# Causal masking of the first layer's attention: a GpSimd select on the exponentials instead of mask matmuls

## What is computed

```python
q_rope = _rotary_apply(x @ W_q_rope, cos, sin)
scores = jnp.einsum('bqhd,bkhd->bhqk', q, k)
scores = scores + jnp.einsum('bqr,bkr->bqk', q_rope, k_rope)[:, None]
scores = scores / scale
causal = jnp.triu(jnp.ones((Tt, Tt), dtype=bool), k=1)
scores = jnp.where(causal[None, None], -jnp.inf, scores)
w = jax.nn.softmax(scores, axis=-1)
attn = jnp.einsum('bhqk,bkhd->bqhd', w, v).reshape(Bb, Tt, D_MODEL)
return attn @ W_o
```

## Time and profile before

| | us |
|---|---|
| median of 3 runs | 988.91 |
| lowest, highest | 984.66, 989.62 |
| the profiled execution | 987.88 |
| its span, first to last instruction | 986.1 |
| first layer's attention, quads 4 to 63 | 93.9 to 322 |
| dense experts | 322 to 560 |
| second layer's attention | 580 to 845 |
| routed experts and output | to 986 |

### The profile page before, as it was taken

One profiled execution on the slowest core, in us unless ns is written; L12 is line 12 of the kernel. 1 busy time (PEld: TensorE's weight loads), 2 busy tenths in 40 slices (PEclk: granted clock), 3 DMA queues, 4 the chain that ended last, 5 costly groups with the idle time before them and its releaser, 6 DMA issues. The chain is left out here.

```text
span 986.1 us, 13424 instructions
## 1 busy us (share of the span) xinstructions
PE 817.1 (83%) x4532; PEld 519.6 (53%) x4532; DVE 657.8 (67%) x1354; ACT 521.0 (53%) x938; POOL 289.5 (29%) x227
## 2 busy tenths in 40 slices
PE   3567999999998899999989899789889999527850
PEld 2234555665564677777767644345444444226740
DVE  3135567676664586776867697688998886347852
ACT  1013455555546677777767626556556566317740
POOL 3452530311300100000004264772453452133425
PEclk9999999999999999999999969989999999859985
DMA  4253211111110292000002103210010100011003
GB/s 128 47 94 80 72 34 35 34 27 41 31 23 1 80 285 63 0 1 1 1 9 54 46 1 101 63 34 18 26 37 18 47 15 7 6 54 57 31 33 85
DMA packets 56415, 44.84 MB, mean 45 GB/s; under 512 B 6598, under 2 KB 47259, under 8 KB 56347
## 3 DMA queue, kind: packets, MB, share of 16 engines
q1 hardware_dynamic: 55323, 41.88, 16.3%
q0 software_dynamic: 1024, 2.10, 0.7%
HBM read 14.73 MB, written 14.55 MB: 30 GB/s over the span
## 5 line engine op out<-in xcount | busy, mean ns | idle before, releaser
L881 ACT ACTIVATE ring<-single 128x512 f32<-128x512 f32 (+3 forms) x512 | 255.6, 517 | 261.3 <-PE single L1084 143.6
L1496 DVE TENSOR_REDUCE mneg<-pair 128x2 f32<-128x1024 f32 (+3 forms) x256 | 259.6, 1022 | 84.4 <-PE pair L1084 55.7
L1082 PE MATMUL single<-q_op,k_op 104*128 104x512 f32 (+3 forms) x512 | 223.4, 449 | 15.5 <-ACT ring L881 10.7
L1082 PE MATMUL pair<-k_op,q_op 96*128 96x512 f32 (+3 forms) x512 | 185.3, 436 | 31.7 <-DVE mneg L1496 17.5
L747 POOL TENSOR_SCALAR k_op<-k_stk,cst 104x512 fp32r<-104x512 f32 x64 | 99.7, 1573 | 272.1 <-DMA k_stk<-hl 254.5
L1082 PEld LDWEIGHTS single<-q_op,k_op 122*128 122x128 f32 (+1 forms) x512 | 100.6, 197 | 91.6 <-ACT ring L881 65.0
L1082 PEld LDWEIGHTS pair<-k_op,q_op 120*128 120x128 f32 (+1 forms) x512 | 106.1, 212 | 49.2 <-DVE mneg L1496 25.0
L1140 PE MATMUL p_o<-ring,vaug 128*9 128x512 f32 (+3 forms) x1024 | 116.4, 527 | 0.9 <-ACT ring L881 0.9
L908 ACT ACTIVATE ring<-pair,cols 128x512 f32<-128x512 f32 x136 | 86.0, 684 | 35.3 <-PE pair L1184 29.6
L1551 DVE TENSOR_TENSOR ring<-ring,single 128x1024 f32<-128x1024 f32 x60 | 73.3, 1221 | 46.0 <-ACT ring L908 44.8
L1556 DVE TENSOR_TENSOR hid_lo<-ring,hid_hi 128x1024 fp32r<-128x1024 f32 x68 | 84.1, 1237 | 22.7 <-ACT hid_hi L923 19.7
(11 more groups left out here) (293 smaller groups left out, 1301.1 us busy)
## 6 DMA issues: line engine op xcount, KB each, us to landing
xs<-zero SPq DMA_DIRECT2D x10, 1024.0 KB, 10.2
q_op<-hl SPq DMA_DIRECT2D x96, 64.0 KB, 2.0
stage<-in_L_ffn_W_dram SPq DMA_DIRECT2D x8, 512.0 KB, 4.4
stage<-in_L_ffn_rW_dram SPq DMA_DIRECT2D x6, 512.0 KB, 5.8
k_op<-hl SPq DMA_DIRECT2D x48, 64.0 KB
...
```

The lines of the kernel that those rows point to most:

```text
L881: exp_done.by(act.activation(ring[:, n % 8, lo:T], singles[n % 2][:, lo:T], ACT.Exp), (L, n))
L1082: ins = pe.matmul(dst[:, lo:hi], r32(lhs[:, lhs_lo:lhs_lo + P]), r32(rhs[:, lo:hi]), start=True, stop=L == 1)
L1496: s_taken.by(dve.tensor_reduce(mneg[:, G % 2, qt, 2 * p:2 * p + 2], pairs[m % 2][:, :, 0:hi], axis=AX.X, op=ALU.max, negate=True), (L, m))
```

## The change

- Exp units of the first layer lose their mask matmul. The upper triangle of the diagonal tile gets an unmasked exponential, and POOL then sets it to 0: cut_half(Q, half) is one affine_select over two heads' diagonal tiles in ring, 128 partitions x 2 x 128, in place. It waits for the second of its two exponentials. values(Q) waits for the second select of its quad instead of the last exponential.
- values(Q - 1) stands behind exp unit 2 instead of exp unit 1 in the first layer, behind the parts "b". ACT's out_rows stands behind the fourth exponential instead of before it.
- Max units with qt 0 or 1, whose two heads have 256 columns each, write both heads into one bank. One mask matmul of 2 x 128 columns serves both. Units with qt 2 or 3 stay as they were.
- POOL's work is interleaved: behind each half quad's select stands at most one step, a quarter of a rope_copy (two heads of q or k) or a third of a piece of weights (the rounded copy, and the subtraction in two halves). Before, the first four pieces were split ahead of quad 0, and all by quad 10; now it begins in quad 3 and ends in quad 23. The piece loads on SP's queue are spread accordingly between the transfers of operands and maxima.
- The table B_MT goes, and the constants are 128 columns narrower.

The diff, cut to its core:

```diff
+WEIGHT_STEP = {at: n for n, at in enumerate([(0, k) for k in (*range(6, 16), *range(20, 24), *range(28, 32))]
+                                            + [(1, k) for k in range(4, 16)])}
...
+        def unit_scores(L, m):
+
+            pair = pairs[m % 2]
+            return pair[:, 0, :].rearrange("p (i k) -> p i k", i=2) if L == 0 and m % 4 < 2 else pair[:, :, :]
...
             for r in range(NB):
                 G = NG * r
                 m_dma(0, G + 1)
+                head_dma(G + 3)
                 if r == 0:
-                    for n in range(4, 8):
-                        expert0(n)
-                head_dma(G + 3)
+                    expert0(4)
                 if r < NB - 1:
                     rope_dma(r + 1)
+                if r == 0:
+                    expert0(5)
                 m_dma(0, G + 2)
                 if r == 0:
-                    for n in range(8, len(PIECE0)):
-                        expert0(n)
+                    expert0(6)
                 if r < NB - 1:
                     head_dma(G + 4)
                 m_dma(0, G + 3)
+                if r == 0:
+                    expert0(7)
                 if r < NB - 1:
                     head_dma(G + 5)
+                    if r == 0:
+                        expert0(8)
                     m_dma(0, G + 4)
                     head_dma(G + 6)
+                if r == 0:
+                    expert0(9)
...
-            def rope_copy(G):
+            def rope_copy(G, w, half):
                 r, s = G // NG, G % 3
-                pool.wait_ge(rope_rows, R_ROWS * (r + 1))
-                if G >= 3:
-                    exp_done.wait_ge(pool, (0, 16 * (G - 3) + 15))
-                apart(pool)
-                dst = slice(GH * s, GH * s + GH)
-                pool.tensor_copy(r32(q_op0[0:96, dst, :]), qk_rope[:, 0:1, :].broadcast_to([96, GH, T]))
-                rope_set.by(pool.tensor_copy(r32(k_op0[0:96, dst, :]), qk_rope[:, 1:2, :].broadcast_to([96, GH, T])), G)
-
-            def weights0(n):
+                if (w, half) == (0, 0):
+                    pool.wait_ge(rope_rows, R_ROWS * (r + 1))
+                    if G >= 3:
+                        exp_done.wait_ge(pool, (0, 16 * (G - 3) + 15))
+                    apart(pool)
+                at = GH * s + 2 * half
+                ins = pool.tensor_copy(r32((q_op0, k_op0)[w][0:96, at:at + 2, :]), qk_rope[:, w:w + 1, :].broadcast_to([96, 2, T]))
+                if (w, half) == (1, 1):
+                    rope_set.by(ins, G)
+
+            def weights0(n, step):
                 which, lo, hi = PIECE0[n]
-                pool.wait_ge(staged0[n % 4], 16 * (n // 4 + 1))
-                src = stage0[:, n % 4, 0:hi - lo, :]
-                steps.step(pool.tensor_copy(r32(w0[:, which, 0, lo:hi, :]), src))
-                split0.by(pool.tensor_tensor(r32(w0[:, which, 1, lo:hi, :]), src, w0[:, which, 0, lo:hi, :], ALU.subtract), n)
+                mid = (lo + hi) // 2
+                if step == 0:
+                    pool.wait_ge(staged0[n % 4], 16 * (n // 4 + 1))
+                    apart(pool)
+                    steps.step(pool.tensor_copy(r32(w0[:, which, 0, lo:hi, :]), stage0[:, n % 4, 0:hi - lo, :]))
+                elif step == 1:
+                    pool.tensor_tensor(r32(w0[:, which, 1, lo:mid, :]), stage0[:, n % 4, 0:mid - lo, :], w0[:, which, 0, lo:mid, :], ALU.subtract)
+                else:
+                    split0.by(pool.tensor_tensor(r32(w0[:, which, 1, mid:hi, :]), stage0[:, n % 4, mid - lo:hi - lo, :], w0[:, which, 0, mid:hi, :],
+                                                 ALU.subtract), n)
...
+            fill = pool.to_reg(0.0)
+
+            def cut_half(Q, half):
+
+                kc = Q % NT
+                exp_done.wait_ge(pool, (0, GH * Q + 2 * half + 1))
+                at = (GH * Q + 2 * half) % 8
+                tri = ring[:, at:at + 2, P * kc:P * (kc + 1)]
+                cut.by(pool.affine_select(tri, tri, [[0, 2], [1, P]], ALU.is_ge, fill, base=0, channel_multiplier=-1), (Q, half))
+
             for G in range(3):
-                rope_copy(G)
-            for n in range(8):
-                weights0(n)
-            rope_copy(4)
-            for n in range(8, len(PIECE0)):
-                weights0(n)
-            rope_copy(5)
-            rope_copy(6)
-            pool.wait_ge(loads[4], n_load[4])
-            pool.tensor_scalar(by_dim(w_q[1][:, :]), by_head(w_qkv[:, 0:D]), SCALE1, None, ALU.mult)
-            pool.tensor_copy(by_dim(w_k1[:, :]), by_head(w_qkv[:, D:2 * D]))
-            pool.wait_ge(cols_ready, 1)
-            pool.tensor_copy(b_cols[:, :, 0:4], cols[:, R_B1:R_B1 + C1].rearrange("p (e c) -> p e c", c=4))
-            pool.tensor_copy(b_cols[:, :, 4:5], cols[:, R_B2:R_B2 + E1].unsqueeze(2)).then_inc(pool_set, 1)
-            for G in (8, 9, 10, 12, 13, 14):
-                rope_copy(G)
+                for w, half in ((0, 0), (0, 1), (1, 0), (1, 1)):
+                    rope_copy(G, w, half)
+            for r in range(NB):
+                for k in range(8 * NG):
+                    cut_half(4 * NG * r + k // 2, k % 2)
+                    if k < 4 and r:
+                        rope_copy(4 * r + 2, k // 2, k % 2)
+                    elif 16 <= k < 20 and r < NB - 1:
+                        rope_copy(4 * r + 4, k // 2 % 2, k % 2)
+                    elif 24 <= k < 28 and r < NB - 1:
+                        rope_copy(4 * r + 5, k // 2 % 2, k % 2)
+                    elif (r, k) in WEIGHT_STEP:
+                        n = WEIGHT_STEP[r, k]
+                        weights0(n // 3, n % 3)
+                    elif (r, k) == (2, 8):
+                        second_weights()
...
-                    if q % NT == 0 and Q:
+                    if L and q % NT == 0 and Q:
                         out_rows(L, Q // NT - 1)
                     for name, b in beside_quad(s, q, "b"):
                         part(name, b)
                     exp(L, Q, 3)
+                    if L == 0 and q % NT == 0 and Q:
+                        out_rows(L, Q // NT - 1)
...
-            def scores(L, dst, lhs, rhs, lhs_lo, lo, hi, diagonal, mask):
-                ins = pe.matmul(dst[:, lo:hi], r32(lhs[:, lhs_lo:lhs_lo + P]), r32(rhs[:, lo:hi]), start=True, stop=L == 1)
-                if L == 0:
-                    ins = pe.matmul(dst[:, diagonal:diagonal + P], id_bf[:, :], bfc[:, mask:mask + P], start=False, stop=True)
-                return ins
...
+                both = unit_scores(L, m)
                 for i in range(2):
                     qs, ks = operands(L, G, 2 * p + i, 24)
-                    ins = scores(L, pairs[m % 2][:, i, :], qs, ks, P * qt, 0, hi, P * qt, B_MS)
+                    ins = pe.matmul(both[:, i, 0:hi], r32(qs[:, P * qt:P * (qt + 1)]), r32(ks[:, 0:hi]), start=i == 0 or L == 1 or qt >= 2, stop=L == 1)
+                    if L == 0 and qt >= 2:
+                        ins = pe.matmul(both[:, i, P * qt:P * (qt + 1)], id_bf[:, :], bfc[:, B_MS:B_MS + P], start=False, stop=True)
+                if L == 0 and qt < 2:
+                    ins = pe.matmul(both[:, :, P * qt:P * (qt + 1)], id_bf[:, :], bfc[:, B_MS:B_MS + P].unsqueeze(1).broadcast_to([P, 2, P]),
+                                    start=False, stop=True)
...
-                st_full.by(scores(L, singles[n % 2], ks, qs, P * kc, lo, T, P * kc, B_MT), (L, n))
+                st_full.by(pe.matmul(singles[n % 2][:, lo:T], r32(ks[:, P * kc:P * (kc + 1)]), r32(qs[:, lo:T]), start=True, stop=True), (L, n))
 
             def values(L, Q):
                 G, kc = Q // NT, Q % NT
-                exp_done.wait_ge(pe, (L, GH * Q + GH - 1))
+                if L:
+                    exp_done.wait_ge(pe, (L, GH * Q + GH - 1))
+                else:
+                    cut.wait_ge(pe, (Q, 1))
...
                         exp_unit(L, Q, j)
+                        if Q and j == (2, 1)[L]:
+                            values(L, Q - 1)
                         if j == 1:
-                            if Q:
-                                values(L, Q - 1)
                             for name, b in beside_quad(s, q, "b"):
...
-                s_taken.by(dve.tensor_reduce(mneg[:, G % 2, qt, 2 * p:2 * p + 2], pairs[m % 2][:, :, 0:hi],
+                s_taken.by(dve.tensor_reduce(mneg[:, G % 2, qt, 2 * p:2 * p + 2], both[:, :, 0:hi],
                                              axis=AX.X, op=ALU.max, negate=True), (L, m))
```

20 lines of the change are left out of this document (14 added, 6 removed).

## The result

The changed kernel takes 1004.3 us (median of 4 runs, 1001.2 to 1005.0) against 986.8 for the kernel before (4 runs, 984.2 to 989.6): a ratio of 1.016, interval 1.013 to 1.019, which is called 16 us below (the medians lie 17.5 apart). The prediction had 970. The profiled run of the changed kernel took 1004.1 us with a span of 1002.4.

The account below looks back on a forecast made before the run. TensorE's instruction stream was taken to bound the first layer's attention. Groups with norms gave 11.9 us, light groups 7.2, groups 2 and 3 nothing, group 0 0.5, less 1 for SP: 18.6 off 987.9, predicted 970, range 955 to 990.

Parts of the forecast that it names:

- the supply: First layer's attention: TensorE time freed by masks removed or merged, 2.3 us a group, 37 us over 16 groups.
- wide quads: First layer's attention: two or three pair units, 0.5 to 0.7 us each, cover the value matmuls' wait for selects.
- the bounds of the select: One GpSimd select over 256 columns: 0.40 to 0.96 us by other GpSimd rows, 0.75 taken.
- SP's order: Expert pieces spread on SP's load queue: one stands ahead of row maxima quad 16 needs, 1 us charged once.
- slow selects: Rival, chance 0.16: GpSimd selects of 1.3 us make the attention slower, 10.6 us lost, 998.
- groups 2 and 3 over 15 us, the selects are slow: Sign in the first layer's attention: these groups, forecast at about 13.8 us, exceeding 15 would mean slow selects.
- the loop binds: Rival, chance 0.09: TensorE's 19.4 us of waits for exponentials grow as masks go; gain under 5 us, 985.
- The moved values: Value matmuls one score matmul later, waiting for the second select: TensorE idles about 0.4 and 0.3 us between key tiles.
- the second rival: VectorE takes over, chance 0.15: queueing reductions eat 1 us more of each group with norms; gain 11.6, 977.
- GpSimd's second price: Select latency in the first layer's attention: value matmuls wait for their quad's second select, some 10 us in all.
- The clock is no rival: First layer's attention: clock granted 1.00 with TensorE 95% busy, 90% expected after; no clock loss charged.
- the move of the copy of p_o: ScalarE's 0.59 us copy, behind key tile 0's fourth exponential: TensorE waits about 0.4 us once a group.

Follow-up runs that it names:

- the kernel with the one reduction: The changed kernel with the rounded maxima mrow written by a one-element maximum (TENSOR_REDUCE) instead of a copy: 995.3 us, ratio 1.0078 to the kernel before.
- The kernel free of the port wait: The changed kernel with four one-input reductions in place of the copy and subtraction that split the turned maxima: 993.4 us, ratio 1.0061 to the kernel before.

## Why the prediction was wrong

**What held.** The place of the supply; that value matmuls would be covered in wide quads; the bounds of the select (0.407 within 0.40 to 0.96, though 0.75 was taken); the stages outside. SP's order cost nothing where 1 us was charged: no row of the stage waits for a transfer. The rival with the right sign, slow selects at 998, came near the measured time by luck, for a reason that is false: by the prediction's own sum the measured 0.407 should have given 960. So the sign "groups 2 and 3 over 15 us, the selects are slow" misled too: they took 16.7 and 16.8 with fast selects. (The 1.0 us between the profiled run and the median was added to 970 but not to 978 and 998; nothing hangs on it.)

**1. The supply, 2.3 us a group, 37 in all.** In groups at full clock TensorE's busy time falls by 1.5 us a group without the single masks, where 2.0 were counted, and by 0.35 with the two-head masks, about the 0.3 counted: 1.8 a group. The step from a distance between neighbours in a packed row to 16 a group was the error, since a mask ahead of a value matmul or a wait has another price. The larger error was the overlap: the sum let nearly all of it through, and of the 1.5 only 0.8 arrived, because TensorE then waited for exponentials and maxima. Over the whole kernel 7 us came from the 256 single masks. The rival "the loop binds" came nearest: it let under 5 us through of 37, and had 0.09.

**2. The moved values, priced at the select's latency only.** The prediction walked what the third score does ahead of the values and forgot what the values had stood in front of: mt, which waits for the split of the maxima. The order alone costs 6 us (ratio 1.0059), and taking it back in the changed kernel brings 12 of 16. VectorE now leads TensorE's waits, which was the sign of the second rival, but that rival had queueing reductions in mind and a kernel faster than before (977); what came is the order and the split.

**3. GpSimd's second price was not the second price.** Throughput and latency of GpSimd were worked out over half the prediction; neither decided. From 89 to 175 us it was busy 53.0 of 86 us, 62% where over 85% was forecast, and value matmuls waited 0.4 us for selects where some 10 were. Its port mattered, which the prediction put at nothing. The trace of before had the sign, one row that wasn't read, VectorE and GpSimd at 103 us:

```profile
103.37 1.97 DVE L1505 CAST mrow<-mneg 128x16 fp32r<-128x16 f32 x1
...
102.95 2.36 POOL L674 TENSOR_TENSOR w<-stage,w 128x1024 fp32r<-128x1024 f32 x1
```

Of 16 copies in the first layer two ran beside a GpSimd instruction. This one took 1.97 us and ended with it (105.34 against 105.31), the other 0.40, and the rest 0.17 or 0.18. In the changed kernel GpSimd works beside eleven of the 16, and they take 0.32 to 2.16 us. A split that GpSimd doesn't hold up brings 10 us (ratio 1.0061 against 1.016).

**4. "The clock is no rival."** By an estimate from rows it was the largest single piece. In groups 6, 7, 10 and 11 the changed kernel ran at 0.89 and took 15.5, 16.0, 15.5 and 16.0 us; the same groups of the kernel with the one reduction ran at 1.00 and took 14.0, 14.1, 14.0 and 14.4. Group 7 of that kernel, to be held against the row of after above:

```profile
198.10:212.20 14.10, 12.27 (x86) 7.12 (x86) 8.43 (x15) 7.41 (x19) 7.08 (x12) 1.00 0.15 30
```

The wait for mrow was 0.35 us shorter there (1.20 against 1.55), the groups 1.5 to 1.9. In groups 8 and 12 it was the other way round. Group 8 of the changed kernel, then of the one with the one reduction:

```profile
219.30:236.50 17.20, 14.33 (x101) 8.64 (x100) 14.26 (x43) 8.27 (x20) 7.10 (x12) 1.00 0.12 26
...
212.20:230.40 18.20, 15.63 (x100) 10.16 (x99) 14.15 (x43) 8.26 (x19) 7.09 (x12) 0.91 0.11 24
```

In group 12 the two took 15.5 us and, at 0.90, 16.8. Here the group with the fall had the slightly shorter wait (1.64 against 1.76, and 1.55 against 1.76) and was still the longer one. With the difference of the waits taken out, a fall made its group 1.1 to 1.6 us longer in the six pairs, 1.3 in the mean; each is 3.4 us at 1.2 GHz. The 37 us are 11 of these, some 14 us. It is how the waits of 2 and 3 became large. The reasoning "TensorE will be 90% busy instead of 95%" was about a mean, while the clock followed single gaps: the one of 2.7 us was followed by 5 us of work at half speed.

**The sum as measured.** In the stage +18.1 us: idle +28.6, busy -27 for the masks (1.8 a group) and, as the rest, some +17 for work at the lower clock. This is an estimate; 37 us at half speed could add 18.7 at most. Of the whole kernel's +16 us (1.6%), 4 are left without the moved order, 6 without the port wait and 6 without the selects. The three overlap and don't add.

**Open.** How much the move of the copy of p_o and the finer load order cost wasn't tried alone; by name TensorE waited 2.7 us for that copy, in 3 pieces. The kernel free of the port wait still stands 0.6% above before, although it has fewer masks than the kernel in which the order alone costs 0.6%; the selects or the remaining falls of the clock take that, and no run separates them. That the clock's fall causes the longer groups is read from pairs of groups, not from a run that held the clock. What decides whether a wait is followed by a fall is open too: one of 1.04 us was, two of 1.76 us were not.
